# Two more K and Q buffers in the memory of the normalised input, and three early maxima in every feed-forward step

## What is computed

```python
xn = _layernorm(x)
# attention: 16 sub-heads of width 8, in pairs that share a V of width 16
q, k = apply_rope(xn @ Wq.T), apply_rope(xn @ Wk.T)
scores = jnp.einsum('bhtd,bhsd->bhts', q, k)
probs = jax.nn.softmax(scores, axis=-1).reshape(b, H, 2, t, t)
diff = probs[:, :, 0] - lam * probs[:, :, 1]
attn = jnp.einsum('bhts,bhsd->bhtd', diff, v)          # then normalised per head, @ Wo.T
# feed-forward: the router picks 3 of 8 zones for each batch row
z = jax.nn.gelu(xn @ Wa[e]) @ Wb[e]                    # for the three zones, weighted
x = x + attention + (xn + weighted sum of z)
```

## Time and profile before

| | us |
|---|---|
| median of 3 runs | 494.6 (494.06 to 495.29) |
| the profiled execution | 494.95 |
| its span, first to last instruction | 493.2 |
| TensorE, VectorE, ScalarE busy | 447.6, 390.6, 305.9 |
| feed-forward steps | about 59 to 177 |
| attention steps | about 177 to 478 |

### The profile page before, as it was taken

How to read it: one execution, slowest core, us unless ns; L and a number is a source line. 1 busy time by engine, 2 the same in 40 slices (tenths; PEclk the granted TensorE clock), 3 DMA queues, 4 the chain that set the end, 5 groups by cost and what they waited for, 6 DMA issues and landing times.

```text
span 493.2 us, 6979 instructions
## 1 busy us (share of the span) xinstructions
PE 447.6 (91%) x2575; PEld 189.8 (38%) x2575; DVE 390.6 (79%) x742; ACT 305.9 (62%) x376; POOL 57.2 (12%) x68
## 2 busy tenths in 40 slices
PE   7496689999999999969999999999999999999987
PEld 5384444454545423322333333333333333232235
DVE  2886668887887879957999999999899989996125
ACT  1431112222222348856978989888888888989972
POOL 4166731101200000000000000000000000000000
PEclk9597879999999989986999999999999999999999
DMA  8407944101000000020002002000100200000002
GB/s 306 185 10 246 348 170 165 44 2 44 1 3 0 1 1 2 2 85 3 0 3 86 3 2 87 1 1 23 66 3 1 86 1 3 1 3 1 1 2 85
DMA packets 12036, 25.62 MB, mean 52 GB/s; under 512 B 1250, under 2 KB 5986, under 8 KB 11874
## 3 DMA queue, kind: packets, MB, share of 16 engines
q1 hardware_dynamic: 11570, 22.37, 13.0%
q10 hardware_dynamic: 432, 2.81, 1.5%
HBM read 15.48 MB, written 9.44 MB: 51 GB/s over the span
## 4 chain that ended last, share of the span: by engine, by line
PE 55%; DVE 19%; ACT 9%; issue 8%; DMA 5%; SPq 2%; POOL 1%; ACTq 0%; DVEq 0%; POOLq 0%
PE ps L946 17%; DVE part_max L665 14%; PE ps L916 14%; PE ps L939 8%; ACT E L504 8%; PE ps L881 7%; DMA X<-in_x 3%; PE ps L800 2%; PE ps L802 2%; PE ps L801 2%; DMA q_scr<-ropeL 1%; DMA Q<-q_scr 1%; PE ps L1013 1%; SPq L292 1%; PE ps L1022 1%
## 5 line engine op out<-in xcount | busy, mean ns | idle before, releaser
L665 DVE TENSOR_REDUCE part_max<-ps 128x1 f32<-128x512 f32 x512 | 317.2, 680 | 50.3 <-PE ps L916 49.4
L504 ACT ACTIVATE E<-ps 128x1024 f32<-128x1024 f32 x256 | 245.6, 1027 | 44.8 <-PE ps L939 43.8
L916 PE MATMUL ps<-K,Q 32*128 32x512 f32 x512 | 160.4, 482 | 9.3 <-DMA Q<-q_scr 3.7
L946 PE MATMUL ps<-E,Vg 128*32 128x512 f32 x1024 | 140.3, 621 | 1.6 <-ACT E L504 1.1
L939 PE MATMUL ps<-Q,K 32*128 32x512 f32 x512 | 120.6, 489 | 7.5 <-ACT E L504 6.3
L916 PEld LDWEIGHTS ps<-K,Q 32*128 32x128 f32 x512 | 69.9, 187 | 140.6 <-DVE part_max L665 120.7
L483 ACT ACTIVATE h<-ps 128x512 f32<-128x512 f32 x48 | 28.7, 597 | 89.5 <-PE ps L802 89.2
L939 PEld LDWEIGHTS ps<-Q,K 32*128 32x128 f32 x512 | 49.4, 186 | 45.1 <-ACT E L504 40.1
L881 PE MATMUL ps<-h,wb_f 128*128 128x512 f32 x96 | 54.0, 646 | 0.0
L426 POOL TENSOR_TENSOR U<-AT,rsum 128x256 f32<-128x256 f32 x15 | 9.3, 621 | 317.7 <-DVE rsum L721 317.7
L800 PE MATMUL ps<-xnH,waH 128*128 128x512 f32 x48 | 37.3, 778 | 0.0
(11 more groups left out here) (131 smaller groups left out, 246.7 us busy)
## 6 DMA issues: line engine op xcount, KB each, us to landing
K<-k_scr SPq DMA_DIRECT2D x8, 512.0 KB, 3.6
Q<-q_scr SPq DMA_DIRECT2D x8, 512.0 KB, 4.6
k_scr<-ropeH SPq DMA_DIRECT2D x6, 512.0 KB, 5.2
tab<-in_tables ACTq DMA_DIRECT2D x1, 2048.0 KB, 10.7
q_scr<-ropeL SPq DMA_DIRECT2D x4, 512.0 KB, 5.8
q_scr<-ropeH SPq DMA_DIRECT2D x4, 512.0 KB, 6.6
wa_raw<-in_wa SPq DMA_DIRECT2D x6, 256.0 KB, 2.8
wb_raw<-in_wb SPq DMA_DIRECT2D x6, 256.0 KB, 3.6
```

Of the source, the lines that this page charges most:

```text
L504: nc.scalar.activation(E[:, par, 2 * jj:2 * jj + 2, :].rearrange("p j t -> p (j t)"), ps[:, 2 * jj:2 * jj + 2, :].rearrange("p j t -> p (j ...
L665: nc.vector.tensor_reduce(part_max[:, tile // FC % 2, j * FC + tile % FC, sh:sh + 1], ps[:, SLOT_BANK[quad_slot(t) + k], :], AX.X, ALU.max ...
L916: mm(ps[:, SLOT_BANK[x], :], Q[strip(j), g % KQ_BUFS, tile % TB * P:(tile % TB + 1) * P], K[strip(j), g % KQ_BUFS, sh * BANK:(sh + 1) * BA ...
L946: last = mm(ps[QUAD * j:QUAD * (j + 1), B_PV, :], Vg[:, par, st, j // 2, :], E[:, s % 2, k, :], start=(st == 0), stop=(st == TB - 1), skip ...
```

## The change

Two things. First, KQ_BUFS becomes 5. Buffers 0 to 2 are the old tiles (KQ_OWN = 3); buffer 3 is xnH (Q in its first half, K in its second) and buffer 4 is xnL in the same way. Groups 3 and 4 are loaded when all 48 first products are made (g1_done), and groups 5, 6 and 7 when groups 0, 1 and 2 have had their last scores. The order of SyncE's queue follows. Second, LEAD_STEPS goes; the 144 early maxima (still 36 quads) are made three in each of the 48 steps, so that quads run over the steps' bounds. The banks of `lead_ring` are told by the maximum's step as before.

```diff
@@ -57,10 +57,11 @@
 ALL_UNITS = GROUPS * UG
 
 QUADS = 2 * GROUPS * TB
-KQ_BUFS = 3
-
-LEAD_STEPS = tuple(n for n in range(UNITS) if n % 4 < 3)
-LEAD = len(LEAD_STEPS)
+
+KQ_OWN, KQ_BUFS = 3, 5
+
+LEAD_BANKS = 3
+LEAD = UNITS * LEAD_BANKS // GJ
 SLOTS = 2 * ALL_UNITS + 2 * GROUPS
 
 MAX_STEPS = 116
@@ -87,11 +88,16 @@
     return min(33 * hx + 36, SLOTS - 1)
 
 
-def lead_ring(t):
+def lead_slots(n):
+
+    return [divmod(x, GJ) for x in range(n * LEAD_BANKS, (n + 1) * LEAD_BANKS)]
+
+
+def lead_ring(t, k):
 
     if t >= LEAD:
         return RING
-    n = LEAD_STEPS[t]
+    n = (GJ * t + k) // LEAD_BANKS
     return (4, 5, 2, 3) if n < 22 else (4, 5, 3, 0) if n < 26 else (4, 5, 0, 1)
 
 
@@ -100,8 +106,8 @@
     banks, before, last = [], [], {}
     for t in range(QUADS):
         extra = (t % 8 == 0 and t > 0) + (t == QUADS - 1)
-        for _ in range(4 + extra):
-            bank = min(lead_ring(t), key=lambda b: last.get(b, -1))
+        for k in range(GJ + extra):
+            bank = min(lead_ring(t, min(k, GJ - 1)), key=lambda b: last.get(b, -1))
             before.append(last.get(bank))
             last[bank] = len(banks)
             banks.append(bank)
@@ -114,8 +120,8 @@
 
 def last_lead_slot(banks, steps=UNITS):
 
-    quads = sum(n < steps for n in LEAD_STEPS)
-    return max(x for x in range(quad_slot(quads)) if SLOT_BANK[x] in banks)
+    t, k = lead_slots(steps - 1)[-1]
+    return max(x for x in range(quad_slot(t) + k + 1) if SLOT_BANK[x] in banks)
 
 
 def max_slots(s):
@@ -174,7 +180,7 @@
             ("identR", [P, P], F32R), ("XN", [P, TILES, P], F32),
             ("V", [P, GROUPS * TB * 2 * QUAD], F32),
             ("xnH", [P, TOKENS], F32R), ("xnL", [P, TOKENS], F32R),
-            ("Q", [P, KQ_BUFS, SEQ], F32R), ("K", [P, KQ_BUFS, SEQ], F32R),
+            ("Q", [P, KQ_OWN, SEQ], F32R), ("K", [P, KQ_OWN, SEQ], F32R),
             ("lam_in", [DQ, 4], F32), ("w1_in", [P, ROUTER], F32), ("b1_in", [ROUTER, 1], F32),
             ("w2_in", [ROUTER, ZONES], F32), ("b2_in", [1, ZONES], F32), ("eps", [P, 1], F32),
             ("stats", [P, TILES, 6], F32), ("mv", [P, TILES, 2], F32), ("rstd", [P, TILES], F32), ("shift", [P, TILES], F32),
@@ -210,6 +216,8 @@
         ones = cst[:, C_ONE:C_ONE + P]
         RES = XN
 
+        Qs = [Q[:, i, :] for i in range(KQ_OWN)] + [xnH[:, 0:SEQ], xnL[:, 0:SEQ]]
+        Ks = [K[:, i, :] for i in range(KQ_OWN)] + [xnH[:, SEQ:], xnL[:, SEQ:]]
         sq = [V1[:, k * BANK:(k + 1) * BANK] for k in range(2)]
 
         k_scr = nc.dram_tensor("k_scr", (GROUPS, P, SEQ), F32, kind="Internal").ap()
@@ -309,14 +317,14 @@
 
             def kq_load(i):
                 sp.sem_inc(sp_waited, 1)
-                sp.dma_start(K[:, i % KQ_BUFS, :].bitcast(F32), k_scr[i]).then_inc(kq_in[i % KQ_BUFS], 16)
-                sp.dma_start(Q[:, i % KQ_BUFS, :].bitcast(F32), q_scr[i]).then_inc(kq_in[i % KQ_BUFS], 16)
+                sp.dma_start(Ks[i % KQ_BUFS].bitcast(F32), k_scr[i]).then_inc(kq_in[i % KQ_BUFS], 16)
+                sp.dma_start(Qs[i % KQ_BUFS].bitcast(F32), q_scr[i]).then_inc(kq_in[i % KQ_BUFS], 16)
 
             def max_rows(hx):
                 i, half = hx // 2, hx % 2
                 sp.wait_ge(slot_read, half_slot(hx) + 1)
                 for part, row in ((maxH, MAX_ROW), (maxL, MAX_ROW + 1)):
-                    dst = Q[row:P:QUAD, i % KQ_BUFS, half * BANK:(half + 1) * BANK].bitcast(F32)
+                    dst = Qs[i % KQ_BUFS][row:P:QUAD, half * BANK:(half + 1) * BANK].bitcast(F32)
                     sp.dma_start(dst.rearrange("j (t c) -> j t c", c=P), part[:, half, :].bitcast(F32)).then_inc(qmax_in, 16)
                 sp.wait_ge(qmax_in, 32 * (hx + 1))
                 sp.sem_inc(sp_waited, 1)
@@ -333,7 +341,7 @@
             sp.wait_ge(scr_out, 48 * 2)
             kq_load(0)
             zones += [picked(e) for e in range(2, PICKS)]
-            for i in range(1, KQ_BUFS):
+            for i in range(1, KQ_OWN):
                 kq_load(i)
             raw_next(0)
             scratch(2)
@@ -346,14 +354,18 @@
             raw_next(3)
             for hx in range(1, 4):
                 max_rows(hx)
-            for i, halves in zip(range(KQ_BUFS, GROUPS), ((4,), (5, 6), (7, 8), (9, 10), (11, 12))):
+            sp.wait_ge(g1_done, UNITS)
+            sp.sem_inc(sp_waited, 1)
+            for i in range(KQ_OWN, KQ_BUFS):
+                kq_load(i)
+            for i, halves in zip(range(KQ_BUFS, GROUPS), ((4, 5), (6, 7), (8,))):
                 for hx in halves:
                     max_rows(hx)
                 sp.wait_ge(st_done[0], 2 * STEPS * (i - KQ_BUFS + 1))
                 sp.sem_inc(sp_waited, 1)
                 sp.wait_ge(st_done[1], 2 * STEPS * (i - KQ_BUFS + 1))
                 kq_load(i)
-            for hx in range(13, 2 * GROUPS):
+            for hx in range(9, 2 * GROUPS):
                 max_rows(hx)
             for k, c in enumerate(TAIL_ORDER):
                 sp.wait_ge(o_done, k + 1)
@@ -702,9 +714,8 @@
             nc.vector.scalar_tensor_tensor(comb[:], cst[:, C_E1:C_E1 + 2 * QUAD], nlc, comb[:],
                                            ALU.mult, ALU.add).then_inc(comb_done, 1)
             for n in range(UNITS):
-                if n in LEAD_STEPS:
-                    for k in range(GJ):
-                        reduce_slot(LEAD_STEPS.index(n), k)
+                for t, k in lead_slots(n):
+                    reduce_slot(t, k)
                 if n % UZ == 2 and n // UZ + 1 < PICKS:
                     wb_zone(n // UZ + 1)
 
@@ -913,8 +924,8 @@
                 if tile % TB == 0 and sh == 0 and k == 0:
                     pe.wait_ge(kq_in[g % KQ_BUFS], 32 * (g // KQ_BUFS + 1))
                 ring_free(x)
-                mm(ps[:, SLOT_BANK[x], :], Q[strip(j), g % KQ_BUFS, tile % TB * P:(tile % TB + 1) * P],
-                   K[strip(j), g % KQ_BUFS, sh * BANK:(sh + 1) * BANK], start=True, stop=True).then_inc(slot_made[j], 1)
+                mm(ps[:, SLOT_BANK[x], :], Qs[g % KQ_BUFS][strip(j), tile % TB * P:(tile % TB + 1) * P],
+                   Ks[g % KQ_BUFS][strip(j), sh * BANK:(sh + 1) * BANK], start=True, stop=True).then_inc(slot_made[j], 1)
                 if k == GJ - 1 and t % TB == 0 and t:
                     half_transpose(t // TB - 1)
 
@@ -936,7 +947,7 @@
 
                 g, th, st, j = n // STEPS, n // TB % 2, n % TB, PLACE[k]
                 rows, buf = strip(j), g % KQ_BUFS
-                mm(ps[:, k, :], K[rows, buf, st * P:(st + 1) * P], Q[rows, buf, th * BANK:(th + 1) * BANK],
+                mm(ps[:, k, :], Ks[buf][rows, st * P:(st + 1) * P], Qs[buf][rows, th * BANK:(th + 1) * BANK],
                    start=True, stop=True).then_inc(st_done[k // 2], 1)
 
             def probs_v(s, par):
@@ -958,11 +969,10 @@
                         pe.wait_ge(wa_split, a // UZ + 1)
                     pe.wait_ge(gelu_done, n + H_LEAD - 1)
                     first(a)
-                if n == LEAD_STEPS[0]:
+                if n == 0:
                     pe.wait_ge(rot_done, 4 * BATCH * CB)
-                if n in LEAD_STEPS:
-                    for k in range(GJ):
-                        max_slot(LEAD_STEPS.index(n), k)
+                for t, k in lead_slots(n):
+                    max_slot(t, k)
                 if n % UZ == 0:
                     pe.wait_ge(wb_done, n // UZ + 1)
                 pe.wait_ge(gelu_done, n + 1)
```

## The result

The changed kernel takes 478.6 us (median of 4 runs, 478.23 to 479.25) against 494.4: 0.968 of before, interval 0.966 to 0.970. The forecast was 480.7 within 477.0 to 486.5. The profiled execution took 479.25 us, its span is 477.5, 15.7 less than before. In the code of after the lines lie eleven or twelve further down: L916 is L927, L881 is L892, L946 is L957, L939 is L950, L665 is L677.

What follows compares the result with a forecast made beforehand. TensorE, busy 91% of the span, was taken as the bound, VectorE mattering where TensorE waits for PSUM banks. Savings of 5.4 (40 steps), 0.1 (ahead of step 4) and 8.4 (stand and clock) sum to 13.9 us: 480.7, range 477.0 to 486.5.

Steps and rivals of the forecast that it cites:

- A step with a free group takes 2.19 us; a group of three costs what four cost: Feed-forward steps: three maxima hold TensorE 0.43 us as four do (bounds 0.32 and 0.64), so plain steps take 2.19 us.
- VectorE keeps pace: Feed-forward steps: three reductions take 1.83 us of 2.19, the bank is read 0.44 us early, so plain cycles never wait.
- 90.6 us for the 40 steps, 2.1 of it for the transposes: Group of step 4 to that of step 44: 87.6 + 0.9 + 2.1 for transposes = 90.6 us, 5.4 less.
- The turn stays at 7.9 us: Group of step 44 to the first score: twelve maxima left in both kernels, so 7.9 us stay.
- The stand and the clock, 8.4 us: Five attention steps from 213.04 us: 19.7 become 11.3 us, 8.4 less: stand 3.7, clock 4.7.
- Ahead of step 4, 0.1 us: Up to the group of step 4: same work in a low-clock slice, so 0.1 us less, between 0 and 1.2.
- The rival "the clock stays low elsewhere": Half clock moves elsewhere, say the turn to attention, costing 4.7 us: 485.4 us; chance 0.14.
- The rival "slower": Mode changes and short waits drop the clock in feed-forward steps; slower from 7 steps on, 507 us with 12; chance 0.02.
- SyncE: Loads of groups 3 and 4: the new wait delays nothing; four transfers land within some 5 us each, hidden by attention steps.

Runs made afterwards that it cites:

- four_and_two: The kernel after, with the same 144 early maxima in groups of four and two in turn instead of three: 0.969 of before.
- same_strip_twice: The kernel after, with each early maximum's matmul issued twice in a row in the same strip and bank: 489.4 us, 0.987 of before.
- more_early: The kernel after, with ten early maxima in each three feed-forward steps (160) instead of nine (144): 476.9 us, 0.962 of before.
- buffers_only: The kernel before with only the five K and Q buffers, keeping four maxima in three of four feed-forward steps: 486.1 us, 0.982 of before.
- warm_stand: The kernel before, with 16 more products into a free bank while TensorE would stand for group 3's load: 488.8 us, 0.988 of before.
- before_again: The kernel before, unchanged, run and profiled a second time: 494.0 us.
- three_only: The kernel before with only three maxima in every feed-forward step, keeping three K and Q buffers: 486.2 us, 0.983 of before.
- four_buffers: The kernel after, with only one more K and Q buffer (in xnH) instead of two: 478.3 us, 0.967 of before.
- lambda_late: The kernel after, with VectorE's chain on lambda moved from ahead of the first maximum to the turn to attention: 477.0 us, 0.962 of before.

## Why the prediction was right, and where its sum was off

*A step with a free group takes 2.19 us; a group of three costs what four cost.* Right, 2.19 and 0.43. It rested on one lone maximum; four_and_two shows it for two and four. same_strip_twice and the seven banks of the attention step show the reason, the strips.

*VectorE keeps pace.* Right: it waits 0.30 us a step, where three reductions at the pace of the earlier trace rows leave 2.19 - 1.83 = 0.36. more_early shows how near the edge that is: a fourth maximum in every third step is enough to be held up.

*90.6 us for the 40 steps, 2.1 of it for the transposes.* 90.45 and 90.44. With 87.6 and 0.9 taken off, the transposes cost 1.9.

*The turn stays at 7.9 us.* Right, 7.89 in after. But before had 9.44 in its second profile, with half clock there.

*The stand and the clock, 8.4 us.* The mechanism is shown by buffers_only and warm_stand; the size was 7.7 and 7.9 in the two pairs of profiles. The term that was off is the five steps without a stand: I took 2.26 a step from long averages, 11.3; they take 11.99. Steps 15 to 19 hold a transpose, the split of its row and the evacuation of a half's result, perhaps more than their share; this wasn't tried. Of the 8.4 the clock was put at 4.7 and the stand at 3.7, and measured are 4.4 and 3.3.

*Ahead of step 4, 0.1 us.* This is the term that was mis-sized. I reasoned that at half clock the same work has to pass anyway, and so gave away what the shorter group of step 1 wins. But that half clock was not fixed: it stood in one profile of before at 64 to 71 us, in buffers_only at 66 to 70, and in before_again and warm_stand, whose matmuls are those of before up to 212 us, not at all. Without it the order alone wins 1.2 us (11.43 to 10.27), the upper bound of this term. With it, as in the first pair, 4.0. The 9.66 of three_only would make it 1.8, but its step 0 starts later, and the later step 0 starts, the less is left of the wait for VectorE's chain on lambda: 10.27, 9.99 and 9.66 us for starts at 59.90, 60.81 and 61.28. With step 0 at 59.38 in both, the second product of step 1 starts at 65.10 in before_again and at 63.92 in more_early, again 1.2 us. Where before doesn't have it there, it has it at the end of the feed-forward steps, 1.5 us (9.44 to 7.90).

The later step 0 of after, 1.4 us, goes with the clock too, and not with the change. The half clock ahead of it lasted 3.4 us in before (53.9 to 57.3) and 6.8 in after (51.9 to 58.7), and TensorE's program is the same up to there. buffers_only, with the groups of before, starts step 0 at 60.93, and more_early at 59.38. So by the absolute time of step 4's group the first pair differs by 2.7 us (73.47 and 70.80) and the second by 0.6 (70.81 and 70.17).

In the first pair the sum's shortfall is 3.9 us ahead of step 4, 0.1 from the 40 steps and 0.4 behind step 19, less 1.4 from the later step 0, 0.7 from the turn's longer half clock and 0.7 from the stand. By the unrounded marks that is 1.8 of the 15.7 us, which were not forecast. That the total came so close owes something to luck: terms that were off by 4.4 and by 2.8 us cancel in part, and most of both hangs on where the half clock stood in one execution. I should have given the place its 1.2 us and taken a low clock ahead of it as something that may go.

*The rival "the clock stays low elsewhere"* came true in small: at the turn the half clock lasts nearly 7 us in after (171.4 to 178.2) where it lasted 3.4 in before, and the first score to step 14 takes 0.5 to 0.65 us more. It did not cost 4.7. Nor is it tied to the new order or to the loads: four_buffers, three_only and lambda_late, all with that order and the last with all the loads of after too, have 3.4 us there. Half clock behind one and the same stand lasted nearly 14 us in both profiles of before and nearly 7 in three_only, with TensorE busy almost throughout (at least 1.49 us of every 2). What sets these lengths is left open.

*The rival "slower"*, a low clock within the feed-forward steps, did not come: the granted clock is 1.00 from 60 to 170 us in after. The Trainium skill describes a clock that swings with short idling between groups ("TensorE: Matmul & The Clock Gate", A second HAM failure mode). After doesn't test this, since its groups leave TensorE no such gap (busy 2.00 of 2.00 us in every stretch from 90 to 100 us); before, with groups held up by 0.2 to 0.9 us, kept 1.00 from 72 to 180 us and doesn't bear it out.

*SyncE.* Its new wait held nothing back. The four transfers left together at 164.3 to 165.6 us and landed 3.7 to 6.9 us after their issue, the last later than the 5 I gave, with 35 us to spare. That group 4's load had not been late, and so its buffer bought nothing, could have been read beforehand from the steps I gave for groups 5 to 7.

## What to carry to other kernels

In these steps matmuls in different strips of rows cost by the round and not by the piece: a round of one to four takes the same 0.42 to 0.44 us, so count rounds and the banks that a round needs at once, and spread the work so that its reader never falls behind. A single wait of TensorE can cost more afterwards than while it lasts, here 3.3 us of waiting and 4.4 of half clock, so look for it in the granted clock before looking for busy time. Take a term that sits in a stretch of low clock with the stretch and without it, and profile twice before building on where such a stretch stands.

## What the hardware showed beyond that

Sixteen needless matmuls into a free bank (3.92 us of work in the place of a wait) made the kernel before 5.9 us faster; 4.4 us of it lie between steps 14 and 19, where the clock stayed up. And two profiles of one unchanged program had a low-clock stretch in different places, at 64 to 71 us in one and at 172 to 176 in the other, with a span that differs by 1.0 us.
